# First attention of a two-layer kernel, written out in full: keys projected for four batches at a time from split operands, values projected from 128-row context tiles and moved to their batch by DMA

## The chip, the cores and the metric

One core of one Trainium2 chip runs the whole program. The metric is the device time of one execution in microseconds (us), the median of three runs.

## What is computed

Batch 32, 128 rows of queries (S) of width 128 (D), 77 context rows per batch (KL). The first attention has 16 heads of width 64.

```python
x = x + attention0(layernorm(x), ctx, ctx)    # 16 heads of 64, rope on queries and keys, mask per batch
x = x + ffn0(layernorm(x))                    # int4-rounded 128x128 weight, bias, lora
x = x + attention1(layernorm(x), ctx, ctx)    # 16 heads of 8, biases, one mask
x = x + ffn1(layernorm(x))                    # ternary weights, rounded rows, silu(gate) * up
# attention0:
Q = q @ Wq; K = k @ Wk; V = v @ Wv            # [b, rows, 16, 64]
Q, K = rope(Q), rope(K)
attn = softmax(where(mask == 0, -1e9, (Q / 8) @ K^T))
out = (attn @ V).reshape(b, s, 1024) @ Wo
```

## The kernel before

Each engine has its own instruction stream, written by hand in the order in which it is to run; semaphores tie the streams together. The change touches the first attention only (and where some later buffers lie). It goes over the 32 batches in **slots**, one for each batch b; two slots make a **pair** p (b = 2p + j). Pairs 0, 1, 14 and 15 are written out, pairs 2 to 13 run as six turns of a hardware loop (`pairs_loop`). While a slot computes the attention of its batch, it also prepares the next pair: queries in the even slot, keys in the odd slot, values in both.

In PSUM two banks (`pa`) serve the projections in turn, three (`ps`) the scores, three (`po`) the value products and the output. A projection **task** is: TensorE (PE) waits until its `pa` bank is free, multiplies into it, and another engine reads it out and frees it.

- **X task** (`transposes`): the two normalised x tiles of a pair and their two context tiles are transposed. ScalarE (ACT) copies them out as high parts, VectorE (DVE) makes the low parts.
- **Q tasks** (`project_queries`), four to a pair: a split product of three F32R matmuls (hi·hi, hi·lo, lo·hi; lines 949 to 951) with 256 columns, twice. DVE multiplies by the cosine and shuffles lanes (L665, L668), GpSimd (POOL) multiplies by the sine and adds (L580, L581), ACT casts to bf16 (L850).
- **K tasks** (`project_keys`), three to a pair, of 3, 3 and 2 head-pair tiles: one plain f32 matmul of 154 columns for each tile (L970, two instructions). The first two groups go over DVE (L679, L681) and POOL (L592, L593) with 462 columns; the third, with 308 columns, is rotated by DVE alone (`rope_last_keys`, L717 to L724). ACT casts all three to bf16 (L858).
- **V tasks** (`project_values`), four to a pair: for one batch and half of the heads, a split product with 77 stationary columns and 512 moving ones. ACT copies it to `vs` (L845).

For batch b the slot then runs: `scores` in two halves (L1017, then L1021, which adds the row maximum that ACT copied as `fold`, L862), exponentials on ACT (L867), `values` (L1033), normalisation on DVE (L742 to L749), `turn_out` (L1044), `out_projection` (L1053), `residual` (L754). Ahead of the next batch's scores stand `score_maxima` (L986, L995, from the bf16 keys and queries), the maxima on DVE (L736) and `turn_maxima` (L1007). `turn_maxima` writes into bank `ps[0]`, which `fold_in` on ACT must have read before the next `scores` may start.

Of the kernel before, what the change touches and what calls it, by code (L numbers as in the profile page):

```python
# [31 lines left out]
RPAD = 16  # L32

# [72 lines left out]
def later_weights(nc, ctx, t):  # L106
# [10 lines left out]
    t["f1"] = [sb("f1_" + n, [128, FF // 128, 128], F32) for n in ("wg_in", "wu_in", "wd_in")]  # L117
    f0, a1, f1 = t["f0"], t["a1"], t["f1"]
# [131 lines left out]
class LastFfnFront:  # L250
# [5 lines left out]
    def __init__(self, nc, ctx, t):  # L256
# [4 lines left out]
        self.w_q = [sb(n, [128, NC, 128], BF16) for n in ("wg_q", "wu_q", "wd_q")]  # L261
        self.wT = [sb(n, [128, NC, 128], BF16) for n in ("wgT", "wuT", "wdT")]
# [17 lines left out]
    def weight_sum(self, dve, steps, n):  # L280
        dve.wait_ge(self.t["later_in"], self.t["later_all"])
# [120 lines left out]
def layer0_attention(nc, ctx, t):  # L402
# [8 lines left out]
    ctx_in = [sb(f"ctx_in{i}", [KL, 2, D], F32) for i in range(2)]  # L411
# [5 lines left out]
    wq_hi, wq_lo, wv_hi, wv_lo = (sb(n, [128, 1024], F32R) for n in ("wq_hi", "wq_lo", "wv_hi", "wv_lo"))  # L417
    xT_hi, xT_lo = sb("xT_hi", [D, 2 * S], F32R), sb("xT_lo", [D, 2 * S], F32R)
    ctxT = sb("ctxT", [D, 2 * KL], F32)
    ctxT_hi, ctxT_lo = ([sb(f"ctxT_{n}{i}", [D, 2 * KL], F32R) for i in range(2)] for n in ("hi", "lo"))  # L420
    k_turned_all, k_straight_all = sb("k_turned", [128, 924], F32), sb("k_straight", [128, 924], F32)
    turned_all, straight_all = sb("turned", [128, 1536], F32), sb("straight", [128, 1536], F32)
    k_turned, k_straight = ([a[:, 462 * i:462 * i + 462] for i in range(2)] for a in (k_turned_all, k_straight_all))
    turned, straight = ([a[:, 512 * i:512 * i + 512] for i in range(3)] for a in (turned_all, straight_all))
    qr = [sb(f"qr{i}", [128, TILES, 2, S], F32) for i in range(2)]
    kr = [sb(f"kr{i}", [128, TILES, 2, KL], F32) for i in range(2)]
    qb_all = sb("qb", [128, 2 * TILES * 2 * S], BF16)
    qb = [qb_all[:, 2048 * i:2048 * i + 2048].rearrange("p (t j s) -> p t j s", t=TILES, j=2) for i in range(2)]
    kb = [sb(f"kb{i}", [128, TILES, 2, KL], BF16) for i in range(2)]
    vs = [sb(f"vs{i}", [KL, 2, H0, DK0 + 1], F32) for i in range(2)]  # L430
# [15 lines left out]
                      out_n=out_n[:].rearrange("p a b -> p (a b)"), oTn=oTn[:].rearrange("p a b -> p (a b)"))  # L446
# [4 lines left out]
    first_weights_in, weights_in, inputs_in = sem("first_weights_in"), sem("weights_in"), [sem(f"inputs_in{i}") for i in range(2)]  # L451
# [9 lines left out]
    weights_split, values_split, hi_ready, ctx_ready = (sem(n) for n in ("weights_split", "values_split", "hi_ready", "ctx_ready"))  # L461
# [6 lines left out]
    TURN, Q_TASK, K_TASK, V_TASK = (0, -1), ((0, 0), (1, 0), (0, 1), (0, 2)), ((1, 2), (0, 3), (1, 3)), ((1, 1), (0, 4), (1, 4), (1, 5))  # L468
    Q_GROUPS = len(Q_TASK)
    K_GROUPS = ((0, 3), (3, 6), (6, 8))  # L470


# [17 lines left out]
    def pairs_loop(engine, slot, steps=None, per=0):  # L490

        for p in (0, 1):
            slot(2 * p, p, p % 2, 0, True)
            slot(2 * p + 1, p, p % 2, 1, True)
        with engine.Fori(1, PAIRS // 2 - 1) as i:
            if steps:
                steps.enter(i, 1, per)
            for half in range(2):
                p = 2 * i + half
                for j in range(2):  # L500
                    slot(4 * i + 2 * half + j, p, half, j, True)
        if steps:
            steps.leave(PAIRS // 2 - 2)
        for p in (PAIRS - 2, PAIRS - 1):
            for j in range(2):
                slot(2 * p + j, p, p % 2, j, p < PAIRS - 1)

    def more_pre(p):

        return not isinstance(p, int) or p + 2 < PAIRS  # L510

    def pair(p, n):

        return isinstance(p, int) and p == n

    def last_pair(p):

        return pair(p, PAIRS - 1)

    def a_count(p, task):  # L520

        return 6 * p + task[1] + 1 - task[0]
# [5 lines left out]
    def sync(sp, second):  # L528
        def load(p, P):
            sp.dma_start(ctx_in[P][:], t["ctx"][bass.ds(2 * p, 2)].rearrange("b k d -> k b d")).then_inc(inputs_in[P], 16)  # L530
            sp.dma_start(mask_in[P][:], t["mask0"][bass.ds(2 * p, 2)].rearrange("b s k -> s b k")).then_inc(inputs_in[P], 16)

        load(0, 0)
# [5 lines left out]
        load(1, 1)  # L539
# [4 lines left out]

        def slot(b, p, P, j, more):
            if j == 0 and more:

                load_next(p, P)

        def load_next(p, P):  # L550
            if isinstance(p, int) and p + 2 >= PAIRS:
                return
            sp.wait_ge(a_free[0], a_count(p, TURN) + 1)
            load(p + 2, P)

        pairs_loop(sp, slot)

    def gpsimd(pool, second):
        steps = Steps(pool, pool_step)
        for i in range(2):  # L560
            nc.gpsimd.memset(am[i][:, :, KL:CROW], 0.0).then_inc(setup, 1)
            nc.gpsimd.memset(vs[i][:, :, :, DK0:DK0 + 1], 1.0).then_inc(setup, 1)
# [7 lines left out]
        def rope_turn(p, P, k):  # L570

            if pair(p, 0) and k == 3:
                pool.wait_ge(first_turned, 1)
            else:
                pool.wait_ge(a_free[Q_TASK[k][0]], a_count(p, Q_TASK[k]) + 1)
# [24 lines left out]
        for k in range(2):  # L600
            rope_keys(0, 0, k)
        pre(1)

        def slot(b, p, P, j, more):
# [6 lines left out]
            elif more:  # L611
                for k in range(2):
                    rope_keys(p + 1, 1 - P, k)
                if pair(p, PAIRS - 2):
                    t["start"].deviation(pool, 0)

        pairs_loop(pool, slot, steps, 12)

    def vector(dve, second):
        steps = Steps(dve, dve_step)  # L620

        def masks(p, P):

            dve.wait_ge(inputs_in[P], 32 * (p // 2) + 32 if isinstance(p, int) else (p - P) * 16 + 32)
# [27 lines left out]
        def split_turned(p, P):  # L652

            dve.wait_ge(hi_ready, p + 1)
# [1466 lines left out]
```

## Time and profile before

| | |
|---|---|
| median of 3 runs | 739.62 us (737.15 to 739.86) |
| span of the profiled execution | 736.9 us |
| PE busy | 695.7 us (94% of the span) |
| DVE, ACT, POOL busy | 561.1, 407.2, 403.7 us |
| share of PE in the chain that ended last | 83% |

The span runs from the first to the last instruction of one profiled execution; its own time lies with the runs, and the median of the runs stands 2.7 us above the span. The first attention takes the time from about 34 us (first scores) to about 460 us. "Chain" below is the chain of work that ended last, followed back from the end: each piece is named by its start, its length and what ran.

### The profile page before, as it was taken

The numbers are of one execution on the slowest core, as the hardware profiler recorded it, in microseconds if no ns is written. First come the engines' busy times: TensorE is split into PE (matmuls) and PEld (weight loads), VectorE is DVE, ScalarE is ACT, GpSimd is POOL, SyncE is SP. The second block draws the span as 40 slices with busy tenths as digits, with TensorE's granted clock in tenths as the row PEclk, the third lists the DMA queues.
The fourth block names the chain that finished last, engine by engine and source line by source line (L and its number), as shares of the span: only waits on it lengthen the run. The fifth ranks groups of instructions, "written<-read, shape, count | busy, mean of one in ns | idle before, by whom it ended". The sixth has DMA issues, their size and how long they took to land.

```text
span 736.9 us, 24302 instructions
## 1 busy us (share of the span) xinstructions
PE 695.7 (94%) x9267; PEld 574.1 (78%) x9272; DVE 561.1 (76%) x1633; ACT 407.2 (55%) x902; POOL 403.7 (55%) x496
## 2 busy tenths in 40 slices
PE   3789999999999999999999999999999999997785
PEld 3578888888888888888888887788888888875544
DVE  5676786786786786787787675777887888887996
ACT  2344554544544544545544544556666766766896
POOL 3474574484484474475466452546556565633775
PEclk9899999999999999999999999999999999999999
DMA  9400000000000000000000000000000000000011
GB/s 264 115 9 12 9 3 11 10 0 9 9 0 9 9 0 9 9 0 9 9 0 0 1 2 11 10 7 11 7 9 4 9 4 4 5 2 1 22 44 52
DMA packets 23682, 13.04 MB, mean 18 GB/s; under 512 B 6560, under 2 KB 22768, under 8 KB 23632
## 3 DMA queue, kind: packets, MB, share of 16 engines
q1 hardware_dynamic: 22816, 12.00, 6.1%
q8 instruction: 33, 0.54, 0.3%
q10 hardware_dynamic: 816, 0.36, 0.2%
q14 instruction: 17, 0.14, 0.1%
HBM read 10.25 MB, written 2.10 MB: 17 GB/s over the span
## 4 chain that ended last, share of the span: by engine, by line
PE 83%; DVE 9%; issue 3%; ACT 3%; DMA 1%; POOL 0%; ACTq 0%; SPq 0%; DVEq 0%
PE bank L1017 9%; PE bank L1033 9%; PE bank L1053 8%; PE bank L1648 6%; PE bank L949 5%; PE bank L1021 5%; PE bank L970 4%; PE bank L1681 4%; PE bank L951 4%; PE bank L950 4%; PE bank L1044 4%; PE bank L986 2%; PE bank L1666 2%; PE bank L995 2%; DVE f_h_max L1898 2%
## 5 line engine op out<-in xcount | busy, mean ns | idle before, releaser
L580 POOL TENSOR_TENSOR a_turned<-a_turned,a_rope 128x512 f32<-128x512 f32 x63 | 80.7, 1280 | 175.8 <-DVE a_turned L668 175.8
L867 ACT ACTIVATE a_probs<-bank 77x512 f32<-77x512 f32 x128 | 70.8, 590 | 64.9 <-PE bank L1021 64.0
L845 ACT COPY a_vs<-bank 77x512 f32<-77x512 f32 x64 | 37.4, 584 | 101.5 <-PE bank L951 101.5
L665 DVE TENSOR_TENSOR a_straight<-bank,a_rope 128x512 f32<-128x512 f32 x63 | 43.4, 689 | 58.3 <-PE bank L951 54.5
L581 POOL TENSOR_TENSOR a_qr<-a_straight,a_turned 128x512 f32<-128x512 f32 x64 | 82.3, 1286 | 4.9
L1017 PE MATMUL bank<-a_qr,a_kr 64*77 64x128 f32 x1024 | 71.4, 279 | 2.2 <-ACT a_probs L867 0.3
L1017 PEld LDWEIGHTS bank<-a_qr,a_kr 64*77 64x77 f32 x1024 | 56.5, 145 | 16.4 <-ACT a_fold L862 8.6
L1033 PE MATMUL bank<-a_vs,a_probs 77*64 77x65 f32 x2048 | 67.0, 223 | 0.4 <-DVE x_all L754 0.4
L1033 PEld LDWEIGHTS bank<-a_vs,a_probs 77*64 77x64 f32 x2048 | 62.4, 137 | 4.5 <-DVE x_all L754 0.6
L1053 PE MATMUL bank<-a_wo,a_oTn 128*128 128x128 f32 x512 | 64.0, 278 | 0.0
L736 DVE TENSOR_REDUCE a_am<-bank 128x6 bf16<-128x462 f32 (+1 forms) x96 | 50.3, 581 | 14.2 <-PE bank L995 14.2
L1053 PEld LDWEIGHTS bank<-a_wo,a_oTn 128*128 128x128 f32 x512 | 59.9, 192 | 1.0
L850 ACT CAST a_qb<-a_qr 128x512 bf16<-128x512 f32 x64 | 39.4, 618 | 23.5 <-POOL a_qr L581 23.2
L668 DVE STREAM_SHUFFLE a_turned<-bank 128x512 f32<-128x512 f32 x63 | 46.2, 733 | 0.0
L970 PE MATMUL bank<-a_ctxT,a_wk 128*128 128x154 f32 x256 | 45.0, 312 | 0.7 <-ACT a_vs L845 0.7
L1380 DVE TENSOR_REDUCE a_max_m<-bank 128x8 f32<-128x512 f32 x64 | 41.1, 684 | 5.1 <-PE bank L1629 4.6
L1518 ACT ACTIVATE a_qr<-bank 128x512 f32<-128x512 f32 (+1 forms) x96 | 43.8, 538 | 1.0 <-PE bank L1666 1.0
L949 PE MATMUL bank<-a_xT_hi,a_wq_hi 128*128 128x256 f32 x128 | 40.0, 313 | 3.0 <-DVE a_turned L668 1.6
L1021 PE MATMUL bank<-a_fold,a_fold_w 112*77 112x128 bf16 x512 | 41.1, 223 | 0.0
L593 POOL TENSOR_TENSOR a_kr<-a_k_straight,a_k_turned 128x462 f32<-128x462 f32 x32 | 38.5, 1202 | 4.3 <-DVE a_k_turned L688 1.9
L858 ACT CAST a_kb<-a_kr 128x462 bf16<-128x462 f32 (+1 forms) x48 | 24.2, 533 | 27.8 <-POOL a_kr L593 27.7
L873 ACT COPY a_oTn<-bank 128x512 f32<-128x512 f32 x64 | 35.5, 582 | 7.2 <-PE bank L1044 7.2
(277 smaller groups left out, 1890.2 us busy)
## 6 DMA issues: line engine op xcount, KB each, us to landing
out<-x_all SPq DMA_DIRECT2D x16, 128.0 KB, 1.8
x_all<-in_x_dram SPq DMA_DIRECT2D x7, 256.0 KB, 6.5
a_ctx_in<-in_ctx SPq DMA_DIRECT2D x16, 77.0 KB
a_mask_in<-in_mask SPq DMA_DIRECT2D x16, 77.0 KB
a_wv<-in_ctx SPq DMA_DIRECT2D x16, 77.0 KB
a_wq<-in_Wq SPq DMA_DIRECT2D x1, 512.0 KB, 4.9
a_wk<-in_Wk SPq DMA_DIRECT2D x1, 512.0 KB, 6.3
a_wv<-in_Wv SPq DMA_DIRECT2D x1, 512.0 KB, 7.2
```

Of the source, the lines that this page charges most:

```text
L580: steps.link(nc.gpsimd.tensor_tensor(tv, tv, rope[:, 1:2, :].broadcast_to([128, 4, S]), ALU.mult))
L581: nc.gpsimd.tensor_tensor(qr[P][:, 2 * k:2 * k + 2, :, :].rearrange("p t j s -> p (t j) s"), sv, tv, ALU.subtract if made else ALU.add).th ...
L668: nc.vector.stream_shuffle(turned[k % 3][:], pv, mask=[lane ^ 1 for lane in range(32)]).then_inc(a_free[bk], 1)
L736: nc.vector.tensor_reduce(rows, ps[bk][:, 0:n * KL].rearrange("p (h k) -> p h k", k=KL), AX, ALU.max).then_inc(s_free[bk], 1)
L867: nc.scalar.activation(probs[:, 4 * g:4 * g + 4, :], ps[ST_BANK[g]][0:KL, :].rearrange("p (h s) -> p h s", s=S), ACT.Exp).then_inc(s_free[ ...
L949: nc.tensor.matmul(out, lhs_hi, rhs_hi, start=True, stop=False)
L970: last = nc.tensor.matmul(pa[bk][:, 2 * KL * i:2 * KL * i + 2 * KL], wk[:, 128 * (lo + i):128 * (lo + i) + 128], ctxT[:], start=True, stop ...
L1017: nc.tensor.matmul(ps[ST_BANK[g]][0:KL, i * S:(i + 1) * S], kr[P][e:e + 64, h // 2, j, :], qr[P][e:e + 64, h // 2, j, :], start=i == 0, st ...
L1021: last = nc.tensor.matmul(ps[ST_BANK[g]][0:KL, i * S:(i + 1) * S], fold_w[:, h, :], fold[:], start=False, stop=True, skip_group_check=True)
L1033: last = nc.tensor.matmul(po[r][rows, VW * i:VW * (i + 1)], probs[:, PROBS_SLOT[h], rows], vs[P][:, j, h, :], start=True, stop=True)
L1053: last = nc.tensor.matmul(po[2][:, 0:D], oTn[:, i, :], wo[:, i, :], start=i == 0, stop=i == TILES - 1)
L1648: return nc.tensor.matmul(SCORES[g][:, i * S:(i + 1) * S], keys[P][FEATURES[half], j, 128 * tile:128 * tile + 128], q1[P][FEATURES[half], ...
```

## The change

The hardware loop is gone: all 32 slots are written out (`slots`), with constants in every wait.

Contexts are loaded by **quads** of four batches (308 rows as tiles of 128, 128 and 52 rows). `ctxT_hi` and `ctxT_lo` hold two quads (616 columns), so the plain f32 copy `ctxT` is gone; `wk` is split as well, on ACT and DVE before the first keys.

K tasks: from quad 1 on, a task is one head-pair tile for four batches, a split product of 308 columns (three matmuls); eight to a quad. All eight are rotated by DVE (multiply, shuffle) and POOL (multiply, add); no group is left to DVE alone. Which slot runs which task stands in `KEY_SLOT`. One cast on ACT (`cast_keys`) makes the bf16 keys of one batch and waits for all tasks of its quad; `score_maxima` waits for that cast.

V tasks: a unit is one 128-row tile of the 616 context rows of eight batches, in two halves of heads; five units to eight batches (`VALUE_SLOT`: slots 8o-3, 8o-1, 8o+1, 8o+3, 8o+4). ACT copies a unit to one of two stages, and SP moves the rows to their batches' tiles in a ring of five by two or three DMAs from SBUF to SBUF.

The weights of the last FFN now land in the stages after slot 28, and some of its buffers lie in the ring.

```diff
+    KEY_TASKS = [(0, 2 * h, 2 * h + 2, 2 * i, 2 * i + 2) for h in range(2) for i in range(4)]
+    KEY_TASKS += [(q, 0, 4, i, i + 1) for q in range(1, B // 4) for i in range(TILES)]
+    KEY_SLOT = {1: range(4, 8), 2: range(8, 10), 3: range(10, 16)}
+    for q in range(1, B // 4 - 1):
+        KEY_SLOT[4 * q + 1], KEY_SLOT[4 * q + 3] = range(8 + 8 * q, 12 + 8 * q), range(12 + 8 * q, 16 + 8 * q)
...
+    def keys_of(b):
+
+        return 4 + 4 * (b // 2) if b < 4 else 8 + 8 * (b // 4)
...
+        def place_values(u):
+
+            for half in range(2):
+                read(sp, ("V", u, half))
+            last = pieces(u)[-1][0] - RING
+            if last >= 0:
+                sp.wait_ge(values_full, 2 * last + 2)
+            for b, key, row, n in pieces(u):
+                sp.dma_start(vs_rows[b % RING][key:key + n, :], stage[u % 2][row:row + n, :]).then_inc(values_in_place[u % 4], 16)
...
-        def rope_keys(p, P, k):
-            lo, hi = K_GROUPS[k]
-            n = 2 * (hi - lo)
-            if pair(p, 0):
-                pool.wait_ge(first_turned, k + 2)
+        def rope_keys(n):
+            q, first, end, lo, hi = KEY_TASKS[n]
+            made = n in MADE
+            if made:
+                pool.wait_ge(first_turned, 1 + n)
             else:
...
+                read(pool, ("K", n))
+                tv = k_turned[n % 3].rearrange("p (n s) -> p n s", s=KL)
+                steps.link(nc.gpsimd.tensor_tensor(tv, tv, rope[:, 3:4, 0:KL].broadcast_to([128, 4, KL]), ALU.mult))
+            view = lambda a: a.rearrange("p (i r) -> p i r", i=hi - lo)
+            nc.gpsimd.tensor_tensor(kr[q % 2][:, lo:hi, first:end, :].rearrange("p i j s -> p i (j s)"), view(k_straight[n % 3]),
+                                    view(k_turned[n % 3]), ALU.subtract if made else ALU.add).then_inc(k_roped, 1)
...
+        def rope_keys(n):
+            pv = full(dve, ("K", n))[:, 0:QK]
+
+            dve.wait_ge(k_roped, max(n - 2, 0))
...
-        def cast_keys(p, P, k):
-            if k < 2:
-                act.wait_ge(k_roped, 2 * p + k + 1)
-            else:
-                act.wait_ge(a_free[K_TASK[k][0]], a_count(p, K_TASK[k]) + 1)
-            lo, hi = K_GROUPS[k]
-            nc.scalar.copy(kb[P][:, lo:hi], kr[P][:, lo:hi]).then_inc(cast_done, 1)
+        def cast_keys(b):
+
+            act.wait_ge(k_roped, keys_of(b))
+            nc.scalar.copy(kb[b % 2][:], kr[b // 4 % 2][:, :, b % 4, :]).then_inc(cast_done, 1)
...
         def score_maxima(b, P, j):
+            pe.wait_ge(cast_done, b + 1)
```

**GpSimd, slots 2 and 3** (`a0_kr` are the rotated keys, `a0_qr` the rotated queries, `a0_rstd` the deviation of a later pair). Before, from the last query task of the even slot to the end of the odd slot:

```order
L580 TENSOR_TENSOR a0_turned<-a0_turned,a0_rope 128x512
L581 TENSOR_TENSOR a0_qr0<-a0_straight,a0_turned 128x512
L568 TENSOR_TENSOR a0_rstd<-a0_var,minus_half 128x2
L592 TENSOR_TENSOR a0_k_turned<-a0_k_turned,a0_rope 128x462
L593 TENSOR_TENSOR a0_kr0<-a0_k_straight,a0_k_turned 128x462
L592 TENSOR_TENSOR a0_k_turned<-a0_k_turned,a0_rope 128x462
L593 TENSOR_TENSOR a0_kr0<-a0_k_straight,a0_k_turned 128x462
```

The same place now, on the same engine:

```order
L702 TENSOR_TENSOR a0_turned<-a0_turned,a0_rope 128x512
L703 TENSOR_TENSOR a0_qr0<-a0_straight,a0_turned 128x512
L690 TENSOR_TENSOR a0_rstd<-a0_var,minus_half 128x2
L714 TENSOR_TENSOR a0_k_turned<-a0_k_turned,a0_rope 128x308
L716 TENSOR_TENSOR a0_kr1<-a0_k_straight,a0_k_turned 128x308
```

The last two rows stand there eight times in a row (tasks 8 to 15, all of quad 1), and four times in each later odd slot; before it was two such pairs with 462 columns in every odd slot.

**TensorE, from the values of an odd slot to the next scores** (`a_vs` the values, `a_am` the mask with the row maxima, `a_kb` the bf16 keys, `a_ctx_in` the context rows). Before:

```order
L1033 MATMUL bank<-a_vs,a_probs 64x65 x32
L949 MATMUL bank<-a_wv_hi,a_ctxT_hi 77x512
L950 MATMUL bank<-a_wv_lo,a_ctxT_hi 77x512
L951 MATMUL bank<-a_wv_hi,a_ctxT_lo 77x512
L986 MATMUL bank<-a_am,identb 128x308
L986 MATMUL bank<-a_am,identb 128x462 x2
L995 MATMUL bank<-a_kb,a_qb 128x77 x16
```

and after one more V task, the X task and `turn_out` (L1044):

```order
L1007 MATMUL bank<-identb,a_am 112x128
L949 MATMUL bank<-a_wv_hi,a_ctxT_hi 77x512
L950 MATMUL bank<-a_wv_lo,a_ctxT_hi 77x512
L951 MATMUL bank<-a_wv_hi,a_ctxT_lo 77x512
```

Now the end of that stretch reads (slot 3, then slot 4's first scores):

```order
L1071 MATMUL bank<-a_wv_hi,a_ctxT_hi 128x512
L1072 MATMUL bank<-a_wv_lo,a_ctxT_hi 128x512
L1073 MATMUL bank<-a_wv_hi,a_ctxT_lo 128x512
L1063 MATMUL bank<-ident,a_xhat 128x128 x2
L1066 MATMUL bank<-ident,a_ctx_in 128x52
L1176 MATMUL bank<-ident,a_out_n 128x128 x8
L1136 MATMUL bank<-identb,a_am 112x128
L1146 MATMUL bank<-a_qr,a_kr 77x128 x8
```

The V task between `turn_maxima` (L1007, now L1136) and the scores is gone; the other two of the odd slot keep their places around `score_maxima`, with 128 stationary columns in place of 77.

**ScalarE, an even slot.** Before, `fold_in` (L862) stood behind the copy of a V task:

```order
L850 CAST a_qb<-a_qr 128x512
L845 COPY a_vs<-bank 77x8x64
L862 COPY a_fold<-bank 112x128
L850 CAST a_qb<-a_qr 128x512 x2
```

Now it stands ahead of any V copy:

```order
L966 CAST a_qb<-a_qr 128x512
L975 COPY a_fold<-bank 112x128
L966 CAST a_qb<-a_qr 128x512
L961 COPY a_stage<-bank 104x8x64 x2
L966 CAST a_qb<-a_qr 128x512
```

## Rows read from the trace of the kernel before

**Rows 1.** The page: busy time by engine; shares of the last chain.

```profile
PE 695.7 (94%) x9267; PEld 574.1 (78%) x9272; DVE 561.1 (76%) x1633; ACT 407.2 (55%) x902; POOL 403.7 (55%) x496
...
PE 83%; DVE 9%; issue 3%; ACT 3%; DMA 1%; POOL 0%; ACTq 0%; SPq 0%; DVEq 0%
```

**Rows 2.** The last chain in order of time: start, us, what.

```profile
191.83 2.02 PE bank L1033 x64
...
200.67 0.12 PE bank L950
...
209.05 0.38 PE bank L949
209.44 0.23 PE bank L950
...
210.41 0.27 ACT a_fold L862
...
212.40 0.84 PE bank L970 x6
...
214.11 0.79 PE bank L970 x6
...
216.50 0.58 PE bank L970 x4
...
218.87 2.02 PE bank L1033 x64
...
224.82 0.06 PE bank L1007
...
225.58 1.03 PE bank L1017 x16
```

**Rows 3.** Groups by line and shape: count | busy us, mean ns | idle before.

```profile
L850 ACT CAST a_qb<-a_qr 128x512 bf16<-128x512 f32 x64 | 39.4, 618 | 23.5 <-POOL a_qr L581 23.2
L593 POOL TENSOR_TENSOR a_kr<-a_k_straight,a_k_turned 128x462 f32<-128x462 f32 x32 | 38.5, 1202 | 4.3 <-DVE a_k_turned L688 1.9
...
L592 POOL TENSOR_TENSOR a_k_turned<-a_k_turned,a_rope 128x462 f32<-128x462 f32 x30 | 32.6, 1086 | 0.0
...
L1508 ACT CAST a_wk<-a_turned 128x640 bf16<-128x640 f32 x16 | 11.6, 728 | 0.2
...
L247 POOL TENSOR_TENSOR x_all<-x_all,f_bias 128x256 f32 x10 | 7.3, 727 | 12.9 <-DVE s_xhat L235 12.9
```

**Rows 4.** Timeline of pair 6, slots 12 and 13: start us, us, engine, line.

```profile
209.98 0.42 DVE L749 TENSOR_TENSOR a_out_n<-bank,a_rec 128x256 f32<-128x256 f32 x1
...
210.73 0.69 DVE L665 TENSOR_TENSOR a_straight<-bank,a_rope 128x512 f32<-128x512 f32 x1 [0.33 <-PE bank L951]
...
215.43 1.12 POOL L592 TENSOR_TENSOR a_k_turned<-a_k_turned,a_rope 128x462 f32<-128x462 f32 x1
216.62 1.23 POOL L593 TENSOR_TENSOR a_kr<-a_k_straight,a_k_turned 128x462 f32<-128x462 f32 x1
...
220.17 0.93 ACT L858 CAST a_kb<-a_kr 128x462 bf16<-128x462 f32 x2 [1.71 <-POOL a_kr L593]
...
221.56 0.70 PE L986 MATMUL bank<-a_am,identb 128*128 128x308 bf16 x3
```

**Rows 5.** The last chain, the setup and slot 29.

```profile
28.93 0.70 PE bank L986 x3
...
425.45 0.38 PE bank L949
...
435.27 1.57 PE bank L1033 x48
```

**Rows 6.** Stretches: us, busy us of each engine (count), PE clock, DMA.

```profile
24.00:28.00 4.00, 2.65 (x9) 1.54 (x8) 3.85 (x12) 0.97 (x3) 2.33 (x2) 1.00 0.39 73
...
30.00:32.00 2.00, 1.79 (x7) 0.74 (x4) 1.81 (x5) 0.30 (x1) 0.07 (x1) 0.50 0.46 126
```

**Rows 7.** DMA issues: count, KB each, us to landing.

```profile
x_all<-in_x_dram SPq DMA_DIRECT2D x7, 256.0 KB, 6.5
```

More of the change, by code:

```diff
@@ new lines, in read, with contexts_of, context_task @@
+    def read(engine, name):
+        engine.wait_ge(a_free[TASK[name][0]], TASK[name][1] + 1)
+    def contexts_of(name):
+        if name == ("X", 0):
+            return ((0, 0), (0, 1))
+        if name == ("C",):
+            return ((0, 2), (1, 0), (1, 1), (1, 2))
+        c, odd = (name[1] + 2) // 2, name[1] % 2
+        if odd:
+            return ((c, 2),) if 1 < c < B // 4 else ()
+        return ((c, 0), (c, 1)) if c < B // 4 else ()
+    def context_task(c, i):
+        return next(name for name in TASK if name[0] in "XC" and (c, i) in contexts_of(name))
@@ new lines, in runs_of, with rows_of, value_rows, pieces @@
+    def runs_of(name):
+        out = []
+        for c, i in contexts_of(name):
+            at = c % 2 * QK + 128 * i
+            if out and sum(out[-1]) == at:
+                out[-1] = (out[-1][0], out[-1][1] + rows_of(i))
+            else:
+                out.append((at, rows_of(i)))
+        return out
+    def rows_of(i):
+        return min(128, QK - 128 * i)
+    def value_rows(u):
+        return min(128, 8 * KL - 128 * (u % VT))
+    def pieces(u):
+        r, end, out = 128 * (u % VT), 128 * (u % VT) + value_rows(u), []
+        while r < end:
+            stop = min(end, (r // KL + 1) * KL)
+            out.append((8 * (u // VT) + r // KL, r % KL, r - 128 * (u % VT), stop - r))
+            r = stop
+        return out
@@ L473, in layer0_attention, with placed, tiles_of @@
+    def placed(u):
+        return 16 * sum(len(pieces(v)) for v in range(u % 4, u + 1, 4))
+    def tiles_of(b):
+        first = VT * (b // 8)
+        return [u for u in range(first, first + VT) if any(piece[0] == b for piece in pieces(u))]
+    def keys_of(b):
+        return 4 + 4 * (b // 2) if b < 4 else 8 + 8 * (b // 4)
     SM_BANK = (1, 2, 0)
@@ L488, in layer0_attention, with slots @@
     HALVES = (slice(0, S // 2), slice(S // 2, S))
[L490 to L506, printed above, removed]
+    def slots(slot):
+        for b in range(B):
+            slot(b, b // 2, b // 2 % 2, b % 2, b < B - 2)
     def more_pre(p):
-        return not isinstance(p, int) or p + 2 < PAIRS
+        return p + 2 < PAIRS
     def pair(p, n):
-        return isinstance(p, int) and p == n
+        return p == n
     def last_pair(p):
-        return pair(p, PAIRS - 1)
-    def a_count(p, task):
-        return 6 * p + task[1] + 1 - task[0]
+        return p == PAIRS - 1
     def x_chunk(i):
@@ L610, in slot @@
                     pre(p + 2)
[L611 to L617, printed above, removed]
+            for n in KEY_SLOT.get(b, ()):
+                rope_keys(n)
+            if j == 1 and pair(p, PAIRS - 2):
+                t["start"].deviation(pool, 0)
+        slots(slot)
     def vector(dve, second):
@@ L815, in slot @@
                     next(second)
-                if more:
-                    rope_last_keys(p + 1, 1 - P)
+                for n in keys[2:]:
+                    rope_keys(n)
                 residual(b - 1)
@@ new lines, in project_queries, with project_keys @@
+                last.then_inc(a_full[TASK["Q", p, k][0]], 1)
+        def project_keys(n):
+            q, first, end, lo, hi = KEY_TASKS[n]
+            for i in range(3):
+                if 128 * i < KL * end:
+                    read(pe, context_task(q, i))
+            bank, wide = empty(pe, ("K", n)), KL * (end - first)
+            some = slice(q % 2 * QK + KL * first, q % 2 * QK + KL * end)
+            for i in range(lo, hi):
+                cols = slice(128 * i, 128 * i + 128)
+                last = split_product(bank[:, wide * (i - lo):wide * (i - lo) + wide], wk_hi[:, cols], wk_lo[:, cols],
+                                     ctxT_hi[:, some], ctxT_lo[:, some])
+            last.then_inc(a_full[TASK["K", n][0]], 1)
```

444 lines of the change are left out of this document (248 added, 196 removed).

## Prediction

> **What bounds the kernel now.** I read the page first: PE is busy for 94% of the span and makes 83% of the last chain [rows 1]. The chain in order of time then shows what a pair of slots costs: the values of slot 11 start at 191.83 and those of slot 13 at 218.87, one pair apart by 27.04 us [rows 2], and between them nearly every piece is PE. So PE's own instructions set the pace, and a task taken from PE pays in full, but only until another engine is late. The timeline of the odd slot [rows 4] shows who comes next: the bf16 keys leave ACT at 220.17 + 0.93 = 221.10, and PE's score maxima, which need them, start at 221.56. Keys reach ACT by way of DVE and POOL. That margin of 0.46 us is the thinnest, and the change lengthens just this path.
>
> **PE's work, per pair.** From start to start a split product of 256 columns costs 0.12 us a matmul and one of 512 columns 0.23 [rows 2]; 308 columns lie between them at 0.142. A K task is then 3 x 0.142 + 0.05 for starting a group, 0.47 us, four to a pair: 1.85 (two of the four follow f32 work and need less). Before: 0.84 + 0.79 + 0.58 = 2.21 [rows 2]. Gain 0.36.
>
> V tasks: the first after other work costs 0.38 + 0.23 + 0.24 = 0.85 [rows 2], two in a row 1.55. The odd slot keeps its V task ahead of `score_maxima` and the one behind it. An even slot loses its V task (0.85, of which 0.15 comes back since the query task behind it now pays the start), except in slots 4, 12, 20 and 28, which have two (+0.70). I take 128 stationary columns at the price of 77: the 256-column products already have 128 of them and run at 0.12, so the load hides.
>
> In the even slot PE also waits a little for `fold_in`, which stands behind the V copy: the chain goes over ACT at 210.41 [rows 2]. That goes: 0.2. At the end of the odd slot the V task behind `turn_maxima` goes: from 224.82 to the next scores at 225.58 it was 0.76 [rows 2]. In its place `scores` must wait for `fold_in`, since both use bank `ps[0]`: transposition 0.06, data through 0.15, copy 0.27, wake-up 0.05 each side, about 0.5. Net gain 0.2 to 0.35 (the smaller where the X task has two 128-row tiles).
>
> A pair whose keys are not needed at once thus gains 0.36 + 0.70 + 0.2 + 0.2 = 1.45 us (pairs 4, 8, 12), with two V tasks in the even slot almost nothing, 0.03 (pairs 2, 6, 10).
>
> **The keys' path.** `score_maxima(b+1)` waits for one cast, and that cast for all tasks of its quad. At the end of slots 7, 11, ... 27 the last four of them were started in the same slot. On POOL one such task is a multiply and an add of 308 columns. Rows: 462 columns take 1.086 and 1.202, 256 columns 0.727 [rows 3]; 308 by the two add rows is 0.84, the multiply in the same ratio 0.76, with 0.07 between them (216.62 - 215.43 - 1.12 [rows 4]) and -0.04 to the next: 1.63 a task. The bounds are two thirds of the 462 rows, 1.56, and 1.70.
>
> Laid over the stretch of [rows 4]: the values of the even slot end at 209.05 in both. DVE's normalisation ends at 209.98 + 0.42 = 210.40, and its last query task waits for PE until 210.73; with the V task gone it starts at 210.40, so everything on POOL behind it comes 0.33 earlier, the first key multiply at 215.10 instead of 215.43. The deviation ahead of it keeps its place. Four tasks end at 215.10 + 3 x 1.63 + 1.67 = 221.66. The cast has 616 columns: between 0.618 for 512 and 0.728 for 640 [rows 3], 0.71; with a wake-up of 0.05 on each side PE starts at 222.47. PE itself would be there at 221.56 - 1.26 = 220.30 (0.36, 0.70 and 0.2 from above). So it stands for 2.2 us, and the pair is slower by 0.91 up to this point, faster by 0.35 behind it: +0.56 for pairs 3, 5, 7, 9 and 11; pair 13 has no deviation to make (0.7 less on POOL): -0.1.
>
> Pair 1 is worse. Slot 2 starts two K tasks and slot 3 six, all of quad 1, needed at the end of slot 3. DVE's statistics now stand behind the two tasks in slot 2, and the first of those waits for nothing but the second for a bank until the last query task is read, so the deviation is made about 0.7 later than above, and the tasks start at T + 6.5 (T, the end of the values of slot 2). Eight of them take 7 x 1.63 + 1.67 = 13.1, cast and wake-ups 0.8: score maxima at T + 20.4. Before it was 221.56 - 209.05 + 0.07, T + 12.6. Cost 7.8, less 0.35: +7.45. POOL is never starved on the way: with three buffers DVE is held back by POOL, not the other way.
>
> Pair 0 (slots 0 and 1) has four K tasks and two V tasks in the even slot, which put the last query task 1 us later: 3 x 1.63 + 1.67 from T + 7.1, cast, T + 14.5: +1.9, less 0.2, +1.7.
>
> Pair 14 had K tasks for pair 15 in slot 29 and has none now. Between 425.45 and 435.27 [rows 5] stand 9.82 us; two V tasks, queries, scores, `turn_out`, scores and projection are 8.15. -1.65, and behind the maxima -0.35: -2.0.
>
> **Setup.** SP issues one DMA more ahead of the query weights, and the first X task reads 256 context columns: 0.35 to 0.5 later. DVE makes `wk_lo` (1024 columns) ahead of the first keys, and then four tasks where three stood, the last over POOL; against it, two V tasks are gone from PE between the first score maxima (28.93 [rows 5]) and the first scores. I find the first maxima at 30.5 and the first scores 1.0 later than before, between 0.3 and 1.8.
>
> **The clock.** In the setup PE is busy for 2.65 of 4 us from 24 to 28, and from 30 to 32 its granted clock is 0.50, the 1.2 GHz level [rows 6]. Slot 3 will have like gaps: PE waits some 1.4 us for a bank, 1.5 for the residual (which stands behind the K tasks on DVE) and nearly 3 for the cast. If the clock falls for a few us, that costs 0 to 3.5 us; I take 1.5.
>
> **Sum.** +1.0 (setup) +1.7 +7.45 -0.1 (2, 6, 10) -4.35 (4, 8, 12) +2.8 (3 to 11, odd) -0.1 -2.0 +1.5 = +7.9 us. The profiled execution's span would go from 736.9 to 744.8; the median of the runs lies 2.7 above it, 739.6, so 747.5. The rest of the kernel, the late FFN loads included, is unchanged: those weights are first used in the second attention.
>
> **A page against it.** The POOL rows show 2.35 to 2.6 ns a column at 462 columns (1086/462, 1202/462 [rows 3]). The Trainium skill's "GPSIMD Engine Reference", section 3.1, gives about 2.6 cycles an element at 1.2 GHz for a two-input operation, and says that DVE does the same work about twice as fast, which speaks against handing POOL the third group. By that figure 308 columns take 0.67 us without dispatch, and the sum would come to about no change. The rows are the dearer and decide.
>
> **Rivals.**
> *POOL does not gate; PE alone sets the pace.* Needed is a key task on POOL of 1.1 us (215.10 + 4 x 1.1 = 219.5, cast, 220.3). Then the seven odd pairs gain 1.45 as well: 1.0 + 0.5 (pair 0) - 10 x 1.45 + 1.8 (four more K tasks on PE in pair 1) - 0.1 - 2.0 = -13.3: 726. Against it stand the rows of POOL. 12 in 100.
> *The setbacks are at their low bounds.* 1.56 a task, no clock drop, setup +0.3: 747.5 - 2.3 - 1.5 - 0.7 = 743, and with a shorter queue in slot 3 down to 738. 14 in 100.
> *The values come late.* The unit of slots 3, 11, 19 and 27 is made at the end of the slot and needed in the next one, some 10 us later (scores, three query tasks, maxima, projection: 10.1 by the chain's pieces). Copy 0.7, three issues 1.3, then the transfer: 256 KB took 6.5 us to landing [rows 7], and this is 532 KB in rows of 4160 bytes in SBUF, which no row shows. At 6.5 it is hidden with 1.6 to spare; at twice that PE stands 5 us four times, +20, at 9.5 it is +1.4 each, 753. The Trainium skill's "DMA: Bandwidth & Descriptors", section "Why a DMA increments its semaphore by 16 and not by 1", makes the number of DMA engines the largest divisor of the row count up to 16; the pieces of this unit have 77, 50 and 1 rows, which would spread over 11 and 10 engines, while other pieces (51, 25, 76 rows) have few engines but two slots of time. By that rule the transfer is somewhat slower than a full one. 12 in 100.
> *As forecast.* 62 in 100, own range 744 to 752.
>
> **Chances.** A difference of 0.5% (3.7 us) is about what a measurement of this kernel can tell from no change. The forecast lies wholly above 743.3 save its low edge, so slower: 0.60 + 0.12 = 0.72; same: 0.15; faster: 0.13. The range leaves out the first rival and the dearest end of the third: 739 to 757.
>
> **What the profile would show.** Right: after slots 7, 11, ... the line of `score_maxima` (L1115) waits for ACT's cast (L971), that for POOL (L716), 2 us each, with POOL busy without a break from the last query task; once some 3 us at the end of slot 3. Pairs of 27.6 us and 25.6 us alternate with some of 27.0. V tasks at 0.23 a matmul, K tasks at 0.14. `scores` (L1146) waits 0.3 to 0.4 for `fold_in` at the start of even slots. Wrong: PE without waits at L1115, POOL tasks of much under 1.5 us, or `values` (L1165) waiting for a DMA.

## The result: 763.2 us, 3.3% slower, and the profile after

| | before | after |
|---|---|---|
| median of 4 runs | 739.67 us (737.15 to 739.86) | 763.24 us (762.95 to 767.7) |
| span of the profiled execution | 736.9 us | 761.2 us |
| mean granted clock of TensorE | 0.993 | 0.962 |

The ratio is 1.0327, with a 95% interval of 1.0288 to 1.0367. The sign was forecast and the size was not: 747.5 us was predicted, with a range to 757.

The page of the changed kernel, busy time and shares of the last chain, to be read beside [rows 1]:

```profile
PE 696.1 (91%) x9152; PEld 574.8 (76%) x9152; DVE 549.0 (72%) x1649; ACT 390.2 (51%) x845; POOL 434.1 (57%) x559
...
PE 71%; DVE 11%; POOL 10%; issue 3%; ACT 3%; DMA 0%; SPq 0%; ACTq 0%; DVEq 0%; POOLq 0%
```

PE was to have less to do, and is busy for as long as before (695.7). POOL had no share in the last chain and now has 10%. The first says that PE's instructions got slower, the second that POOL now holds PE up. Both can be seen. First the groups by line and shape (count | busy us, mean ns | idle before):

```profile
L716 POOL TENSOR_TENSOR a_kr<-a_k_straight,a_k_turned 128x308 f32<-128x308 f32 x64 | 53.7, 839 | 5.8 <-DVE a_k_turned L814 0.9
L714 POOL TENSOR_TENSOR a_k_turned<-a_k_turned,a_rope 128x308 f32<-128x308 f32 x61 | 48.0, 786 | 0.6 <-DVE a_k_turned L806 0.5
...
L971 ACT CAST a_kb<-a_kr 128x616 bf16<-128x616 f32 x32 | 22.7, 708 | 51.6 <-POOL a_kr L716 51.6
```

and what PE waited for in the whole span (us in total, times, longest):

```profile
PE bank L1115 <- ACT a_kb L971: 15.6, 9, 2.9
...
PE bank L1146 <- ACT a_fold L975: 5.3, 15, 0.4
PE bank L1136 <- DVE a_am L843: 5.2, 3, 1.7
...
PE bank L1071 <- DVE a_wk_lo L880: 2.5, 1, 2.5
PE bank L1071 <- DVE a_wv_lo L877: 2.1, 1, 2.1
```

No line of the list names the value copies. The chain in order of time through slots 2 and 3 (start, us, what) is POOL's without a gap:

```profile
86.67 0.71 POOL a_rstd L690
87.38 0.78 POOL a_k_turned L714
...
99.84 0.84 POOL a_kr L716
100.68 0.02 issue
100.70 0.71 ACT a_kb L971
101.42 0.05 issue
101.46 1.21 PE bank L1115 x3
```

Eight tasks take 87.38 to 100.68, 1.66 us each. The last row holds the other half of the loss: three matmuls take 1.21 us for which [rows 4] have 0.70. The stretches around it (us; busy us of PE, PEld, DVE, ACT, POOL; granted clock; DMA) say why:

```profile
96.00:98.00 2.00, 1.06 (x18) 0.95 (x19) 1.97 (x7) 0.00 (x0) 1.92 (x3) 1.00 0.00 0
98.00:100.00 2.00, 0.52 (x3) 0.09 (x1) 0.54 (x3) 0.00 (x0) 1.84 (x4) 0.90 0.00 0
100.00:102.00 2.00, 0.54 (x2) 0.28 (x3) 0.00 (x0) 1.19 (x2) 0.67 (x1) 0.50 0.00 0
102.00:104.00 2.00, 2.00 (x20) 1.19 (x19) 0.66 (x2) 0.00 (x0) 0.00 (x0) 0.50 0.00 0
104.00:106.00 2.00, 2.00 (x9) 1.27 (x8) 0.91 (x2) 0.97 (x3) 0.00 (x0) 0.50 0.00 0
106.00:108.00 2.00, 1.65 (x18) 1.45 (x19) 0.54 (x2) 0.97 (x3) 0.00 (x0) 0.90 0.15 46
```

PE waits for the cast and its clock falls to the 1.2 GHz level (0.50). It stays there until some 6.8 us have passed, though PE has work from 101.46 on. The setup shows the same, to be read beside [rows 6]:

```profile
20.00:24.00 4.00, 1.52 (x7) 1.09 (x6) 2.98 (x5) 1.62 (x3) 3.92 (x3) 0.64 0.61 156
24.00:28.00 4.00, 4.00 (x21) 4.00 (x20) 2.91 (x9) 1.24 (x2) 3.58 (x5) 0.50 0.12 19
28.00:32.00 4.00, 3.40 (x12) 1.96 (x12) 3.23 (x15) 1.06 (x2) 2.67 (x4) 0.50 0.01 2
```

A **fall** is from here on such a stretch at the lower clock. The mean clock of 0.962 is 58 us of the span at half speed (761.2 x 0.038 x 2); before it was 10 (736.9 x 0.007 x 2). By stretches of 1 us the falls lie at 21 to 42 (20.5 us) and 48 to 56 (6.8), at the waits at the ends of slots 3 (6.8), 11, 15, 19 (3.4 each) and 27 (6.8), and one at 703 to 711 (6.8) in the last part; before at 29 to 37 (6.8) and one of 3.4 us in the last part.

### The profile page after: what moved, and what is told of

It is laid out like the page before. It is cut to its first block, busy times and chain, and to the rows that moved or that the text cites. A ratio compares the mean times of both kernels' runs of the same rounds, so it can differ in the third digit from the quotient of the medians.

```text
span 761.2 us, 23286 instructions
## 1 busy us (share of the span) xinstructions
PE 696.1 (91%) x9152; PEld 574.8 (76%) x9152; DVE 549.0 (72%) x1649; ACT 390.2 (51%) x845; POOL 434.1 (57%) x559
## 4 chain that ended last, share of the span: by engine, by line
PE 71%; DVE 11%; POOL 10%; issue 3%; ACT 3%; DMA 0%; SPq 0%; ACTq 0%; DVEq 0%; POOLq 0%
PE bank L1146 7%; PE bank L1185 6%; PE bank L1165 6%; PE bank L1784 5%; PE bank L1071 5%; PE bank L1817 4%; POOL a_kr L716 4%; PE bank L1150 4%; PE bank L1072 4%; PE bank L1073 4%; POOL a_k_turned L714 3%; PE bank L1176 3%; PE bank L1115 3%; PE bank L1802 2%; PE bank L1124 2%
## 5 line engine op out<-in xcount | busy, mean ns | idle before, releaser
L961 ACT COPY a_stage<-bank 128x512 f32<-128x512 f32 (+1 forms) x40 | 23.4, 585 | 65.7 <-PE bank L1073 65.3
L716 POOL TENSOR_TENSOR a_kr<-a_k_straight,a_k_turned 128x308 f32<-128x308 f32 x64 | 53.7, 839 | 5.8 <-DVE a_k_turned L814 0.9
L971 ACT CAST a_kb<-a_kr 128x616 bf16<-128x616 f32 x32 | 22.7, 708 | 51.6 <-POOL a_kr L716 51.6
L714 POOL TENSOR_TENSOR a_k_turned<-a_k_turned,a_rope 128x308 f32<-128x308 f32 x61 | 48.0, 786 | 0.6 <-DVE a_k_turned L806 0.5
L1071 PE MATMUL bank<-a_xT_hi,a_wq_hi 128*128 128x256 f32 x128 | 42.0, 328 | 1.8 <-issue 1.6
L1441 POOL TENSOR_TENSOR a_kr<-a_k_straight,a_blocks 128x128 f32<-128x128 f32 x32 | 12.8, 400 | 46.7 <-ACT a_k_straight L1636 46.7
```

What stands on the lines that cost most here:

```text
L716: nc.gpsimd.tensor_tensor(kr[q % 2][:, lo:hi, first:end, :].rearrange("p i j s -> p i (j s)"), view(k_straight[n % 3]), view(k_turned[n % ...
L1071: nc.tensor.matmul(out, lhs_hi, rhs_hi, start=True, stop=False)
```

## Theories and experiments

**Theory A:** POOL's queue of key tasks makes PE wait at the quad ends, and the clock falls behind those waits and behind the two new ones of the setup. **Rival B:** the value copies from SBUF to SBUF are late, or their traffic costs. **Rival C:** the written-out code or the wider tasks are slower on PE by themselves. **Filler** is work for PE whose result nobody reads. Ratios are to the kernel before, run on the same chip.

**Key tasks in other slots.**

```diff
-    KEY_SLOT = {1: range(4, 8), 2: range(8, 10), 3: range(10, 16)}
+    EARLY, KEY_SLOT = {0: (4, 5), 2: range(8, 13)}, {1: (6, 7), 3: range(13, 16)}
     for q in range(1, B // 4 - 1):
-        KEY_SLOT[4 * q + 1], KEY_SLOT[4 * q + 3] = range(8 + 8 * q, 12 + 8 * q), range(12 + 8 * q, 16 + 8 * q)
+        KEY_SLOT[4 * q + 1] = range(8 + 8 * q, 12 + 8 * q)
+        EARLY[4 * q + 2] = range(12 + 8 * q, 14 + 8 * q)
+        KEY_SLOT[4 * q + 3] = range(14 + 8 * q, 16 + 8 * q)
...
                 scores(b, P, j, 0)
+                for n in EARLY.get(b, ()):
+                    project_keys(n)
```

> The same 64 key tasks in other slots: quad 1 gets five at the start of slot 2 and three in slot 3 (was two and six), each later quad four, two and two in slots 4q+1, 4q+2 (at its start) and 4q+3 (was four, none and four). PE's work, POOL's work, the copies and the code's length stay. Theory A (POOL's queue of key tasks holds up the score maxima at the quad ends and in slot 3, and each such wait of PE is followed by a stretch at the 1.2 GHz level): the waits for the cast in slots 3, 7, 11, ... 27 go from 2.1 to 3.4 us to under 0.5, the 48 us at the 1.2 GHz level in 42 to 445 mostly go too, and the median falls by 25 to 38 us, to 725 to 738. Rival B (the values' copies from SBUF to SBUF are late or load the chip) and rival C (the written-out code or the wider tasks are slow by themselves): nothing of theirs changes, 755 to 765.

Measured: 743.5 us, 1.0052 (1.0033 to 1.0071). What PE waited for:

```profile
PE bank L1077 <- DVE a_k_turned L810: 5.8, 10, 0.7
...
PE bank L1121 <- ACT a_kb L977: 1.3, 2, 0.8
```

The wait for the cast fell from 15.6 to 1.3 us and 20 us went, with all of PE's work, copies and code in place. B and C can't explain that. The size that I gave was too large: a new wait of 5.8 us came (query tasks wait for a bank that DVE reads late), and the 20.5 us at the lower clock in the setup stayed. The 48 us at the 1.2 GHz level that the expectation puts between 42 and 445 were misread: the falls listed above add up to 31 there, and 10 are left in this run.

**PE kept busy in the waits for the cast** (`FILL` is 9 at the ends of slots 1, 7, 11, ... 27, and 14 at the end of slot 3).

```diff
         def score_maxima(b, P, j):
+            if b in FILL:
+                pe.wait_ge(s_free[1], SM_COUNT[0](b))
+                for _ in range(FILL[b]):
+                    nc.tensor.matmul(ps[1][:, 0:512], t["identb"][:], am[P][:, 0:1, 0:64].broadcast_to([S, 8, 64]), start=True, stop=True, ...)
             pe.wait_ge(cast_done, b + 1)
```

> PE gets useless work in the waits: nine bf16 matmuls of 512 columns (14 at the end of slot 3) into the bank of the first score maxima, just ahead of the wait for the cast, at the ends of slots 1, 3, 7, 11, ... 27. The waits' length can't fall, since POOL's queue is as before. Theory A with its clock part: the clock stays at 2.4 GHz behind the waits; the stretches at 1.2 GHz behind slots 1, 3, 13 and the others there, 24 to 30 us by the records, half of which is lost time, go: 12 to 15 us off, 748 to 752. If the slow stretches have another cause than PE's idleness (rival): 762 to 766, clock in the slots unchanged.

Measured: 757.1 us, 1.0245 (1.0203 to 1.0287). 6.1 us off by work that nobody needs, half of what I expected: the mean clock is 0.975, the falls of slots 11, 15, 19 and 27 are gone, but the setup's 20.5 us and the 6.8 behind it stay, one of 3.4 us behind slot 3 stays, and a new one of 3.4 us lies at 459 to 463. The filler also overran at two places: at the ends of slots 1 and 3 the maxima start 1.1 and 1.6 us after the cast has ended, where they start 0.05 to 0.2 us after it at the other ends.

**POOL without the multiply by the sine** (the line of L714 left out, so that the keys of tasks 4 to 63 lack this part of their rotation).

> POOL leaves out the multiply by the sine for the keys of tasks 4 to 63 (the keys' turned part is added without it; the only change to what is computed). POOL has some 48 us less to do, a key task on it goes from 1.6 to about 0.85 us, and PE's work is unchanged. Theory A: POOL no longer gates anything, 723 to 732, the sum that I gave for PE alone setting the pace being 726. Rivals B and C: above 750, since copies, code and PE's tasks stay.

Measured: 737.4 us, 0.9964 (0.9942 to 0.9986). POOL doesn't gate (0.6 us of waits for the cast are left), but this is 11 us above the 726 of my rival "PE alone". The clock of 0.977 says that some 34 us still ran at half speed, 20.5 of them in the setup.

**Every value copy made twice.**

```diff
             for b, key, row, n in pieces(u):
+                sp.dma_start(spare[row:row + n, :], stage[u % 2][row:row + n, :]).then_inc(again_in, 16)
                 sp.dma_start(vs_rows[b % RING][key:key + n, :], stage[u % 2][row:row + n, :]).then_inc(values_in_place[u % 4], 16)
```

> Every value copy is made twice, first to a spare tile: 22 units in 2 or 3 pieces more from SBUF to SBUF, the real ones behind them in the queue, and the traffic doubled. Theory A: the copies are hidden with time to spare in most slots, 762 to 766; at worst the four units that are needed one slot later come late by up to 2 us. Rival B (copies late or their traffic costly): 5 to 20 us more, 768 to 783.

Measured: 764.6 us, 1.0341 (1.0295 to 1.0386), the same within the interval as the changed kernel (1.0327), and the waits for the cast are unchanged (15.6 us, 9 times). No wait of PE in the list of this run names a copy either. The interval alone would leave room for some us of cost; the traces don't. Timed from the values of one even slot to those of the next, the pairs without a fall in them agree to 0.04 us (pairs 2, 3 and 4 take 27.34, 27.98 and 25.73 us, in the changed kernel 27.34, 27.94 and 25.74). Pairs 5 and 7 are 1.1 to 1.4 us longer, and there the falls last 6.8 us in place of 3.4. Rival B is out: the copies are hidden even when doubled.

**PE kept busy in the setup alone.** `fill(n)` is n bf16 matmuls of 512 columns into `po[0]`.

```diff
+        fill(9)
         pe.wait_ge(weights_in, WEIGHTS)
         pe.wait_ge(values_split, 2)
         project_values(0, 0)
+        fill(10)
         pe.wait_ge(keys_split, 2)
...
+        fill(4)
         score_maxima(0, 0, 0)
+        fill(7)
         turn_maxima(0, 0, 0)
+        fill(2)
         transposes(("X", 1))
```

> The changed kernel with useless work for PE in the setup alone: nine and ten bf16 matmuls of 512 columns ahead of the waits for the low parts of wv and wk, four, seven and two ahead of the first score maxima, their transposition and the second X task. The waits can't get shorter by it. Clock theory (PE waits 2.1 and 2.5 us there, and the 20 us at the 1.2 GHz level that follow are the consequence): the stretch from 21 to 42 goes, the first scores start at 33 to 35 in place of 36.7, slot 0 is faster by 1 to 2 us, and the median falls by 4 to 8 us, to 755 to 759. If the slow stretch has another cause: 762 to 766.

Measured: 761.8 us, 1.0292 (1.0252 to 1.0332), above what was expected, and not clear of the changed kernel's 1.0327, since the intervals overlap. What follows is read from the two traces. The first half came true: the stretch of 20.5 us shrank to 3.4, and the values of slot 0 start at 43.6 us and not at 47.3. The lead of 3.7 to 4.0 us holds up to slot 10. At slot 12 it is 2.5 and at slot 16 1.5, since behind the waits of slots 11 and 15 the clock now stayed down for 6.8 us where it had been 3.4. The same wait has different prices in two programs whose code differs only in the first 36 us.

**Both of them gone: POOL without the multiply, PE kept busy in the setup** (and `fill(6)` ahead of `turn_maxima` of slot 0).

> POOL leaves out the multiply by the sine for the keys of tasks 4 to 63 (that part of the computation is missing), as in the earlier run that took 737.4, and PE gets the same useless work in the setup as in the run beside it, and six such matmuls ahead of turn_maxima of slot 0. With neither POOL nor the clock in the way only PE's own tasks remain. If my sum for that case (726) was short by the clock alone, and not by PE's tasks: 727 to 731. If PE's tasks in the written-out slots cost more than I took: 734 to 738, though the clock stays at 2.4 GHz.

Measured: 730.9 us, 0.9883 (0.9836 to 0.9929), clock 0.995. With filler the run without the multiply loses another 6.5 us. So PE's tasks are about as cheap as I took them; of the 5 us above 726, pair 1 holds 2.0 (30.1 us for 28.1) and pair 14 1.5 (28.3 for 26.8, with a fall of 3.4 us in it). Rival C is out as the cause of the loss. A small part of it is real: pairs 2, 6 and 10 take 27.3 us here as in the changed kernel, 0.3 more than before, where I had expected no change.

**One of eight tasks rotated by DVE alone**, from quad 2 on: L714, L716 and the shuffle are replaced by two multiplies, a shuffle and a subtraction on DVE for tasks 23, 31, ... 63.

> From quad 2 on, one of the eight key tasks of a quad, the last, is rotated by DVE alone (two multiplies, a shuffle, a subtraction), as the third group was before the change. Theory A: at the ends of slots 7, 11, ... 27 the cast waits for DVE or for one task less on POOL; the wait of 2.1 to 2.4 us falls to 0.3 to 1.2, five or six times, and the slow stretches behind slots 15, 19 and 23 go with it: 10 to 16 us off, 747 to 753. Slot 3 and the setup stay as they are. Rival C (PE's tasks themselves): 760 to 765.

Measured: 749.6 us, 1.0124 (1.0084 to 1.0163). The run is 14 us below the changed kernel: the waits for the cast fall to 4.3 us (three times, 3.0 of it in slot 3), and no fall is left between 105 and 421. Not all of the 14 us is the edit's. The values of slot 6 start 1.8 us earlier than in the changed kernel (141.5 for 143.3), ahead of the first task that was changed (task 23, slot 7), since the falls of the setup and of slot 3 came out 3.4 us shorter each. And a new wait came: `values` for DVE's residual, 5.7 us in 7 pieces (1.3 in 2 before the edit).

**The second V task behind `turn_maxima`**, with the spread key tasks.

> The spread key tasks of the first run (743.5), and the second V task of an odd slot moved behind turn_maxima, where PE otherwise waits 0.35 us for fold_in. Only odd slots with a unit have that task (13 of 15). If the wait for fold_in costs in full: 3 to 4.5 us off, 739 to 741. If turn_maxima then waits longer for the maxima (its wait for DVE is not covered any more): no gain, 742 to 745.

Measured: 744.8 us, 1.0061 (1.0041 to 1.008), no gain over 743.5. PE's wait of `turn_maxima` for DVE's maxima went from 5.2 us (3 times) to 7.4 (10 times): the task had been that wait's cover. The wait for `fold_in` (5.3 us) did go.

**Filler in all the waits.**

> The changed kernel with useless PE work in all the waits: those of the setup, six matmuls ahead of turn_maxima of slot 0, and those ahead of the score maxima at the ends of slots 1, 3, 7, 11, ... 27. POOL's queue gates as before. If my sum was right but for the clock, the pairs come out as I forecast them (27.6, 25.6 and 27.0 us, pair 1 some 34.5) and the median is 747 to 752. If the two fills that took off 6 and 1.5 us by themselves only add up: 755 to 757.

Measured: 751.9 us, 1.0158 (1.0128 to 1.0189), clock 0.993 as before the change. POOL's queue is as in the changed kernel, so this run has the forecast's mechanism with no more clock loss than the kernel before (10.2 us at half speed in both). Its filler overran at the ends of slots 1 and 3. In slot 3 the clock was still down: in the timeline the cast ends at 95.06 + 0.71, and the maxima start at 97.33, 1.5 us later than they could (0.05 us after the cast). In slot 1 the cast ends at 59.44 + 0.71, and the maxima start 1.05 us later than they could.

```profile
59.30 2.12 PE L1116 MATMUL bank<-a_am,identb 128*128 128x512 bf16 x9
59.44 0.71 ACT L971 CAST a_kb<-a_kr 128x616 bf16<-128x616 f32 x1 [4.66 <-POOL a_kr L716]
...
61.25 0.69 PE L1122 MATMUL bank<-a_am,identb 128*128 128x308 bf16 x3
...
93.50 3.99 PE L1116 MATMUL bank<-a_am,identb 128*128 128x512 bf16 x14
97.33 0.69 PE L1122 MATMUL bank<-a_am,identb 128*128 128x308 bf16 x3
```

Without the two it would be about 749.3, an estimate (751.9 less 1.5 and 1.05).

**Key tasks spread evenly** (three in each of slots 0 to 3, two in each later slot), without and with the setup's filler.

```diff
+    EARLY = {0: (4, 5), 2: (10, 11)}
+    KEY_SLOT = {0: (6,), 1: (7, 8, 9), 2: (12,), 3: (13, 14, 15)}
+    for q in range(1, B // 4 - 1):
+        EARLY[4 * q], KEY_SLOT[4 * q + 1] = range(8 + 8 * q, 10 + 8 * q), range(10 + 8 * q, 12 + 8 * q)
+        EARLY[4 * q + 2], KEY_SLOT[4 * q + 3] = range(12 + 8 * q, 14 + 8 * q), range(14 + 8 * q, 16 + 8 * q)
```

> The 64 key tasks spread as evenly as the contexts allow: three in each of slots 0 to 3, two in each later slot up to 27; of the two in an even slot one stands before the first query task and one behind it, in slots 2, 6, 10, ... the first ahead of the scores, where PE waits for fold_in. No filler. Against the first spread (743.5) it takes away PE's waits of 0.3 to 0.8 us for a bank in front of the query tasks and half of the waits for fold_in: 736 to 741. If DVE or the row of maxima becomes late by it: 743 to 748.

> The evenly spread key tasks and the useless PE work in the setup and ahead of turn_maxima of slot 0. By the run without POOL's multiply and with this filler (730.9), in which nothing but PE's tasks is left, and with the waits for fold_in halved: 728 to 732, which would be faster than the kernel before. If the clock falls elsewhere instead: 733 to 738.

Measured: 740.4 us without filler, 1.0004 (0.9988 to 1.002), and 735.7 with it, 0.9941 (0.9921 to 0.9962). The waits for `fold_in` fell from 5.3 to 2.8 us as meant; in front of the query tasks PE still waits 4.9 us in 16 pieces for DVE to free a bank. Of the 5.8 us between the spans of this run and of the one with 730.9, 2.8 stand already at the values of slot 0 (45.9 us for 43.0), ahead of which two key tasks now stand.

**The kernel before with `fill(8)` ahead of its first score maxima.**

> The kernel before with eight such matmuls ahead of its first score maxima, where PE waits 1.8 us and the clock is at the 1.2 GHz level from 29 to 37. If the wait is the cause there too: 1 to 3.5 us off, 736.5 to 739. If not: 739 to 741.

Measured: 737.7 us, 0.9965 (0.9948 to 0.9982): 2 us off. The slow stretch at 29 to 37 is gone and the values of slot 0 start at 41.6 in place of 44.0; a new one of 3.4 us at 43 to 47 gives a part back. Against this version of the kernel before, the best one of the changed kernel (735.7) is ahead by 0.3% only. The intervals of the two ratios overlap, though all six times of the one (734.7 to 735.9) lie below all ten of the other (736.2 to 738.4).

## Why the prediction was wrong

The periods below run from the first value matmul of an even slot to that of the next even one (for the setup: up to that of slot 0, 44.0 us before). Each column is the difference to the kernel before, in us. The last is the run with filler in all waits, less its overrun (1.5 us in pair 1, 1.05 in pair 0); it has as much time at half speed as the kernel before.

| term | forecast | after | clock kept up |
|---|---|---|---|
| setup | +1.0 | +3.4 | -0.6 |
| pair 0 | +1.7 | +4.8 | +2.1 |
| pair 1 | +7.45 | +9.0 | +7.0 |
| pairs 2, 6, 10 | -0.1 | +0.9 | +0.8 |
| pairs 4, 8, 12 | -4.35 | -4.1 | -4.1 |
| pairs 3, 5, 7, 9, 11 | +2.8 | +8.7 | +4.8 |
| pair 13 | -0.1 | +3.2 | +0.6 |
| pair 14 | -2.0 | -1.6 | -0.5 |
| the clock | +1.5 | in the rows above | |
| sum | +7.9 | +24.3 | +10.1 |

**The step that failed** is the one under "The clock": "If the clock falls for a few us, that costs 0 to 3.5 us; I take 1.5." The term was far too small: it had 1.5 us where 11 to 14 were needed. Keeping PE busy in the waits, with the waits themselves left as they are, takes 763.2 to 751.9, or to some 749.3 without the overrun. I had looked for gaps in the setup and in slot 3 and priced one fall. But my own sum put waits of 2.2 us at six more quad ends. It also had DVE make `wk_lo` ahead of the first keys and did not ask how long PE would stand for it: PE waits 2.1 us for `wv_lo` (0.3 at that place before) and 2.5 for `wk_lo`. The kernel before shows what one such wait brings. It waits 1.81 us in the setup, its clock is at the lower level from 29 to 37 [rows 6], and filler in that wait takes this fall away:

```profile
28.93 0.70 PE L986 MATMUL bank<-a_am,identb 128*128 128x308 bf16 x3 [1.81 <-ACT a_kb L858]
```

Each of these places needed the price of a fall. In the pairs it can be read off, since the run with all fillers has the same waits without falls: a fall of 3.4 us made pairs 5, 7 and 9 longer by 1.1 to 1.5 us (29.3 to 29.5 us for 28.0 to 28.2), one of 6.8 us made pair 13 longer by 2.6 (30.2 for 27.7). That is less than half of the fall each time. The rival at the high side, late values, held the range's upper end where this term should have.

**POOL gates: right, and of the size given.** A task takes 1.66 us (forecast 1.63), in rows of 0.79 and 0.84 (0.76 and 0.84), the cast 0.71 (0.71). In pair 5 the values of slot 10 end 2.02 us after 196.98, the maxima start 13.6 us later; the forecast had 13.4 (222.47 - 209.05):

```profile
205.03 0.79 POOL L714 TENSOR_TENSOR a_k_turned<-a_k_turned,a_rope 128x308 f32<-128x308 f32 x1
...
210.97 0.83 POOL L716 TENSOR_TENSOR a_kr<-a_k_straight,a_k_turned 128x308 f32<-128x308 f32 x1
211.83 0.70 ACT L971 CAST a_kb<-a_kr 128x616 bf16<-128x616 f32 x1 [5.47 <-POOL a_kr L716]
...
212.59 1.21 PE L1115 MATMUL bank<-a_am,identb 128*128 128x308 bf16 x3 [1.63 <-ACT a_kb L971]
```

The Trainium skill's "GPSIMD Engine Reference", section 3.1, would have given 0.67 us for 308 columns; both rows are dearer, as [rows 3] had said, and by the page's figure the sum would have come to about no change, where 3.3% was measured.

**PE's own gains: right in the even pairs** (25.5 to 25.7 us for pairs 4, 8 and 12, forecast 25.6), but not in pairs 2, 6 and 10, which are 0.3 us longer each and not 0.03 shorter. Behind the maxima of the odd slots I took 0.35 off; from the maxima at the end of slot 7 (152.61 in the run with all fillers) to the values of slot 8 (165.0) it is 12.4 us, and it was 12.4 before (221.56 to 234.0): nothing was gained there. With the 0.1 by which the maxima come later than forecast that is the excess of the odd pairs, 0.4 each. Pair 13 was taken to have no deviation to make on POOL, 0.7 us less in its queue. It has one, that of pair 15, and so it comes out at +0.6 like the forecast of its neighbours, for -0.1:

```profile
416.26 0.70 POOL L690 TENSOR_TENSOR a_rstd<-a_var,minus_half 128x2 f32<-128x2 f32 x1
```

Pair 14 gained 1.6 of the 2.0 in the changed kernel; the -0.5 of the last column has a fall of 3.4 us in it.

**The setup: its own +1.0 was hidden.** With the clock kept up the values of slot 0 start no later than before (43.4 to 44.0), though against the kernel before with filler (41.6) they are 1.8 later, at my upper bound. What made it +3.4 is the clock behind the two waits for DVE's low parts. Pair 0 comes to +2.1 for +1.7 once the overrun is off: the cast ends 14.8 us after the values of slot 0 (60.15 - 45.36), where the forecast had the maxima at 14.5.

**Values late: not so.** No wait names the copies, and doubling them left the pairs as long as they were where no fall differs.

## What to carry to other kernels

When an engine's wait is forecast, price it twice, if the engine is TensorE and the trace of before shows a fall behind a like wait: the wait itself, and PE's work behind it at half speed for 3.4 or 6.8 us, which was 1.1 to 1.5 or 2.6 us a place in the pairs here. A sum of busy times that comes out lower is no forecast for a change that bunches work on a second engine: the same 64 tasks cost 763 us in bunches of four to eight, and 740 in twos and threes. Before a restructured kernel is compared with its predecessor, let useless matmuls cover the waits of both; it separates what the structure costs from what the clock adds.

## What the runs showed of the hardware

The clock's answer to a wait isn't repeatable from one place to the next. Of six waits for the cast of 1.6 to 2.0 us at the ends of slots 7 to 27 in the changed kernel, four were followed by a fall and two, at slots 7 and 23, were not:

```profile
158.82 0.70 PE L1115 MATMUL bank<-a_am,identb 128*128 128x308 bf16 x3 [1.96 <-ACT a_kb L971]
...
212.59 1.21 PE L1115 MATMUL bank<-a_am,identb 128*128 128x308 bf16 x3 [1.63 <-ACT a_kb L971]
269.18 0.70 PE L1115 MATMUL bank<-a_am,identb 128*128 128x308 bf16 x3 [1.99 <-ACT a_kb L971]
324.37 0.77 PE L1115 MATMUL bank<-a_am,identb 128*128 128x308 bf16 x3 [1.96 <-ACT a_kb L971]
381.01 0.70 PE L1115 MATMUL bank<-a_am,identb 128*128 128x308 bf16 x3 [1.94 <-ACT a_kb L971]
434.52 1.21 PE L1115 MATMUL bank<-a_am,identb 128*128 128x308 bf16 x3 [1.96 <-ACT a_kb L971]
```

The three matmuls take 0.70 us at the 2.4 GHz level and 1.21 at 1.2 GHz. At 269.18 the fall came just behind them, and the shortest wait, at 212.59, had its fall already within it. Nearly all falls of these runs lasted 3.4 or 6.8 us. Those of the changed kernel's setup without filler lasted 17.1 to 23.8. Nor are they the same from one execution to the next: 23 executions of the kernel before on one chip had mean clocks from 0.979 to 0.993 and took 737.9 to 743.9 us. What decides whether a given wait brings a fall stays open. No run here varied the length of a wait by itself.
